# Attention with a lag of three steps: when the products with the values follow the scores, and where the rows of sums are kept

## The reference

```python
def attn(x, Wq, Wk, Wv, Wo, gamma, beta):          # x: 4 x 1024 x 256, 16 heads of 64
    q = jnp.einsum('bsd,hde->bhse', x, Wq)
    k = jnp.einsum('bsd,hde->bhse', x, Wk)
    v = jnp.einsum('bsd,hde->bhse', x, Wv)
    scores = jnp.einsum('bhse,bhte->bhst', q, k)
    scores = jnp.where(causal, scores / jnp.sqrt(jnp.float32(E)), -jnp.inf)
    out = jnp.einsum('bhst,bhte->bhse', jax.nn.softmax(scores, axis=-1), v)
    y = x + out.transpose(0, 2, 1, 3).reshape(B, S, H * E) @ Wo
    return layernorm(y, eps=1e-3) * gamma + beta

def ffn(x, w_gate, w_up, w_down):                  # integer weights times 1/127, 768 hidden
    return (silu(x @ wg.T) * (x @ wu.T)) @ wd.T

x = layernorm(x + attn(x, ...))
x = layernorm(x + ffn(x, ...))
```

## Time and profile before

| | |
|---|---|
| median of 3 runs | 1456.25 us (1454.54 to 1456.58) |
| the profiled execution, its own time | 1458.17 us |
| its span in the trace | 1456.4 us, mean granted clock 0.991 |
| busy: PE / PE weight loads / DVE / ACT / POOL | 97% / 85% / 71% / 69% / 68% of the span |
| instructions: PE / DVE / ACT / POOL | 7976 / 2747 / 1924 / 926 |
| chain that ended last, by engine | PE 73%, ACT 11%, DVE 8%, POOL 4%, issue 3%, DMA 1% |
| POOL's idle time before `probs_lo` (L1428) | 415.1 us, of it 412.5 until ACT's `probs_hi` |
| ACT's idle time before `probs` (L984) | 299.6 us, of it 217.8 until DVE's mask |

### The profile page before, as it was taken

The page is one execution under the profiler, slowest core; times in us unless marked ns, Lnnn a source line. Parts: engine busy times, 40 slices in busy tenths (PEclk is TensorE's granted clock), DMA queues, the critical chain, the costliest instruction groups (busy, mean ns, idle before and its releaser), DMA issues.

```text
span 1456.4 us, 23825 instructions
## 1 busy us (share of the span) xinstructions
PE 1409.0 (97%) x7976; PEld 1231.7 (85%) x7976; DVE 1031.7 (71%) x2747; ACT 1002.1 (69%) x1924; POOL 984.9 (68%) x926
## 2 busy tenths in 40 slices
PE   7899999999999999999999999999999999999876
PEld 6788888888888888888888888888888888888766
DVE  7777776767676766777667676776767677677864
ACT  4777777877676676867668676676767668676534
POOL 4665666556676775867768586775867768588744
PEclk9999999999999999999999999999999999999998
DMA  3323222323342132322243122132313223121000
GB/s 130 102 81 93 62 67 95 117 52 90 103 123 73 52 95 59 110 54 58 74 117 95 52 61 72 56 120 59 95 44 110 74 60 95 51 64 55 23 12 30
DMA packets 61241, 110.46 MB, mean 76 GB/s; under 512 B 16256, under 2 KB 41600, under 8 KB 61120
## 3 DMA queue, kind: packets, MB, share of 16 engines
q1 hardware_dynamic: 61120, 108.94, 25.2%
HBM read 60.95 MB, written 13.89 MB: 51 GB/s over the span
## 4 chain that ended last, share of the span: by engine, by line
PE 73%; ACT 11%; DVE 8%; POOL 4%; issue 3%; DMA 1%; SPq 0%; ACTq 0%; POOLq 0%
PE bank L798 22%; PE bank L771 15%; PE bank L671 8%; PE bank L747 8%; PE bank L734 7%; PE bank L696 5%; PE bank L833 5%; PE bank L845 3%; ACT probs_hi L987 2%; POOL probs_lo L1428 2%; ACT probs L984 2%; ACT y_tail L1023 1%; ACT Q L967 1%; POOL h_lo L1470 1%; ACT K L967 1%
## 5 line engine op out<-in xcount | busy, mean ns | idle before, releaser
L1428 POOL TENSOR_TENSOR probs_lo<-probs,probs_hi 128x512 fp32r<-128x512 f32 x576 | 747.6, 1305 | 415.1 <-ACT probs_hi L987 412.5
L984 ACT ACTIVATE probs<-bank 128x512 f32<-128x512 f32 x576 | 344.2, 598 | 299.6 <-DVE bank L1185 217.8
L771 PE MATMUL bank<-Q,K 128*128 128x512 f32 (+3 forms) x1536 | 385.9, 353 | 3.4 <-ACT probs_hi L987 2.6
L987 ACT ACTIVATE probs_hi<-bank 128x512 fp32r<-128x512 f32 x576 | 342.2, 594 | 0.0
L771 PEld LDWEIGHTS bank<-Q,K 128*128 128x128 f32 x1536 | 252.1, 190 | 33.6 <-ACT probs_hi L987 6.2
L747 PE MATMUL bank<-K,Q 128*128 128x512 f32 (+3 forms) x768 | 245.5, 362 | 3.9 <-DMA Q<-Q 3.3
L1169 DVE CUSTOM_DVE_ANT_0 bank<-bank,mask_keys_free 128x128 f32<-128x128 f32 (+3 forms) x512 | 243.2, 506 | 4.7 <-PE bank L747 4.2
L798 PE MATMUL bank<-probs_hi,VH 128*128 128x512 f32 (+3 forms) x768 | 232.6, 343 | 7.9 <-POOL probs_lo L1428 7.2
L798 PE MATMUL bank<-probs_lo,VH 128*128 128x512 f32 (+3 forms) x768 | 234.7, 346 | 0.0
L798 PE MATMUL bank<-probs_hi,VL 128*128 128x512 f32 (+3 forms) x768 | 234.7, 346 | 0.0
L1185 DVE TENSOR_TENSOR bank<-bank,mask_queries_free 128x256 f32<-128x256 f32 (+1 forms) x320 | 119.4, 373 | 129.4 <-PE bank L771 128.9
(11 more groups left out here) (173 smaller groups left out, 2230.9 us busy)
## 6 DMA issues: line engine op xcount, KB each, us to landing
Q<-Q SPq DMA_DIRECT2D x64, 256.0 KB, 3.7
K<-K SPq DMA_DIRECT2D x64, 256.0 KB, 3.6
recip_bc<-recip_scratch SPq DMA_DIRECT2D x62, 256.0 KB, 3.4
wh<-w_scratch SPq DMA_DIRECT2D x12, 768.0 KB, 4.3
wl<-w_scratch SPq DMA_DIRECT2D x12, 768.0 KB, 5.8
wo_quad<-wo SPq DMA_DIRECT2D x16, 256.0 KB, 2.9
y<-x SPq DMA_DIRECT2D x16, 256.0 KB, 3.8
x_tail<-x SPq DMA_DIRECT2D x13, 256.0 KB, 4.4
```

The lines of the kernel that those rows point to most:

```text
L771: last = mm(bk[:, at:at + cols], KX[:, n, P * i:P * i + P], QX[:, n, q0:q0 + cols], start=(KX is K1 and at == 0), stop=(KX is K2 and at + ...
L984: A(pe_[:, g % 2, :], stb[g % 2][:, :], ACT.Exp).then_inc(exp_done, 1)
L987: A(ph[:, g % RING, :], stb[g % 2][:, :], ACT.Exp).then_inc(hi_done, 1)
L1428: G.tensor_tensor(pl[:, g % RING, :], pe_[:, g % 2, :], ph[:, g % RING, :].bitcast(F32), ALU.subtract).then_inc(lo_done, 1)
```

## The change

- `LAG` goes from 2 to 3 and `RING` from 3 to 4: `pv(g)` is issued at step g + 3, and the tiles of high and low parts have four buffers each. For the last 18 pieces the lag stays 2 (`LAST_LAG`); at step `LAST_AT` + 2 two pieces are multiplied.
- The tile `row_sums` (4 KB in each partition) is gone, which is what the two further buffers take. An odd head's row of sums goes to row 64 of `recip_bc`, with a new wait for the scaling of the pair before. At the end, sums of the last heads go to the tile of a mask, with a wait for the last maximum.
- ACT's `copy_out` moves a step: first half from step 8 of a head to step 0 of the next, second half from step 2 to step 3. DVE's `recip` moves a step with `LAG`.
- SP's sums, stores and loads of reciprocals, one `dup_q` and the load of Wo move by one or two steps, and with it in its queue. `V_AT`, `V_LAST`, the projections, `max_bank` and the scaling stay where they are.

```diff
-LAG, RING = 2, 3
+LAG, RING = 3, 4
+LAST_LAG = 2
...
+def pv_due(g):
+
+    return [i for i, lag in ((g - LAG, LAG), (g - LAST_LAG, LAST_LAG)) if 0 <= i < NG and (i >= LAST_AT) == (lag == LAST_LAG)]
...
-        rsum, RB = sb("row_sums", [P, S]), sb("recip_bc", [P, S])
+        RB = sb("recip_bc", [P, S])
...
-                src = HT[E:E + 1, h // 2 % 3, :] if h % 2 == 0 else rsum[0:1, :]
+                src = HT[E:E + 1, h // 2 % 3, :] if h % 2 == 0 else RB[E:E + 1, :]
...
-                if s == 3 and 1 <= it < NIT:
+                if s == 4 and 1 <= it < NIT:
                     sums(QH * it - 1)
...
-                if s == 5 and 1 <= it < NIT:
+                if s == 6 and 1 <= it < NIT:
                     recip_store(QH * it - 1)
-                if s == 6 and 1 <= it < NIT:
+                if s == 8 and 1 <= it < NIT:
                     recip_load(QH * it - 1)
                 if s == 7 and live:
                     max_to_row(QH * it + 1)
                 if s == 7 and NQ <= nxt < NIT:
                     load_w(nxt)
-                if s == 12 and live:
+                if s == 13 and live:
                     sums(QH * it)
-                if s == 14 and live:
+                if s == 15 and live:
                     recip_store(QH * it)
-                if s == 15 and live:
+                if s == 17 and live:
                     recip_load(QH * it)
...
-                if 0 <= g - LAG < NG:
-                    pv(g - LAG)
+                for i in pv_due(g):
+                    pv(i)
...
                 if (n, c) == (HA, 0):
+
+                    act.wait_ge(mx_read, mx_event_t(NH - 1))
...
-                    A(rsum[own, cols], pvb[n - HA][other, :], ACT.Copy).then_inc(ht_copied, 1)
+                    A(maskS[own, :], pvb[n - HA][other, :], ACT.Copy).then_inc(ht_copied, 1)
...
                     if c == 0:
                         act.wait_ge(sums_loaded, 16 * h)
+                        act.wait_ge(ht_norm, 2 * pair)
+
                     A(HT[E:P, slot, cols], pvb[c][E:P, :], ACT.Copy)
-                    A(rsum[0:1, cols], pvb[c][0:1, :], ACT.Copy).then_inc(ht_copied, 1)
+                    A(RB[E:E + 1, cols], pvb[c][0:1, :], ACT.Copy).then_inc(ht_copied, 1)
...
-                if k == C0_DONE + LAG and 0 <= h < NH - 2:
-                    copy_out(h, 0)
+                if k == C0_DONE + LAG - NS and 1 <= h < NH - 1:
+                    copy_out(h - 1, 0)
```

More of the change, by code:

```diff
@@ L544, in last_recip_load @@
                 sp.wait_ge(recip_stored, 16 * (NH - 1))
-                sp.dma_start(rsum[0:E, CH:S], rscr[HA:HA + 1, 0:CH].partition_broadcast(E).rearrange("e o n -> e (o n)")).then_inc(recip_bc, 16)
+                sp.dma_start(RB[0:E, CH:S], rscr[HA:HA + 1, 0:CH].partition_broadcast(E).rearrange("e o n -> e (o n)")).then_inc(recip_bc, 16)
             def step(g):
@@ L553, in step @@
                         tail_store(XTRA if gset else n, n, gset)
-                if s == 2 and live:
+                if s == 3 and live:
                     dup_q(it, 1)
-                if s == 3 and 1 <= it < NIT:
+                if s == 4 and 1 <= it < NIT:
                     sums(QH * it - 1)
@@ L586, in step @@
                     dup_q(nxt, 0)
-                if s == 21 and live:
+                if s == 22 and live:
                     sums(QH * it + 1)
@@ L590, in step @@
                     dup_k(nxt, 0)
-                if s == 23 and live:
+                if s == 24 and live:
                     recip_store(QH * it + 1)
                     load_wo(it)
-                if s == 24 and live:
+                if s == 26 and live:
                     recip_load(QH * it + 1)
@@ L601, in step @@
                     y_init(it // NQ, Y_INIT_AT.index(s))
-                if s == 30 and 0 <= it < NIT - 1:
+                if s == 31 and 0 <= it < NIT - 1:
                     sums(QH * it + 2)
-                if s == 32 and 0 <= it < NIT - 1:
+                if s == 33 and 0 <= it < NIT - 1:
                     recip_store(QH * it + 2)
@@ L1067, in step @@
                 for h, c in ((NH - 2, 0), (NH - 1, 0), (NH - 2, 1)):
-                    if g == acc_done(h, c) + LAG + 1:
+                    if g == acc_done(h, c) + LAST_LAG + 1:
                         last_copy(h, c)
@@ L1319, in last_norm_c0 @@
                 dve.wait_ge(ht_copied, copies_before(NH - 1, 0) + 1)
-                V.reciprocal(rsum[:, cols], rsum[:, cols]).then_inc(last_recip, 1)
+                V.reciprocal(maskS[:, cols], maskS[:, cols]).then_inc(last_recip, 1)
                 dve.wait_ge(last_recip, 1 + q)
-                V.tensor_tensor(HT[:, slot, cols], HT[:, slot, cols], rsum[:, cols], ALU.mult).then_inc(last_norm, 1)
+                V.tensor_tensor(HT[:, slot, cols], HT[:, slot, cols], maskS[:, cols], ALU.mult).then_inc(last_norm, 1)
             def last_norm_c1(q):
@@ L1329, in last_norm_c1 @@
                     dve.wait_ge(recip_bc, 16 * (NH - 1))
-                    V.tensor_tensor(HT[0:E, slot, CH:S], HT[0:E, slot, CH:S], rsum[0:E, CH:S], ALU.mult)
+                    V.tensor_tensor(HT[0:E, slot, CH:S], HT[0:E, slot, CH:S], RB[0:E, CH:S], ALU.mult)
                     dve.wait_ge(pv_mm, acc_done(NH - 1, 1) + 1)
-                V.reciprocal(rsum[E:P, cols], pvb[HB - HA][0:E, here]).then_inc(last_recip, 1)
+                V.reciprocal(RB[E:P, cols], pvb[HB - HA][0:E, here]).then_inc(last_recip, 1)
                 dve.wait_ge(last_recip, 3 + q)
-                V.tensor_tensor(HT[E:P, slot, cols], pvb[HB - HA][E:P, here], rsum[E:P, cols], ALU.mult).then_inc(last_norm, 1)
+                V.tensor_tensor(HT[E:P, slot, cols], pvb[HB - HA][E:P, here], RB[E:P, cols], ALU.mult).then_inc(last_norm, 1)
             def step(g):
@@ L1368, in step @@
                     last_chain_recip()
-                if g == acc_done(NH - 1, 1) + LAG + 1:
+                if g == acc_done(NH - 1, 1) + LAST_LAG + 1:
                     last_norm_c1(0)
@@ L1388, in step @@
                 for q in range(2):
-                    if g == acc_done(NH - 1, 0) + LAG + 1 + q:
+                    if g == acc_done(NH - 1, 0) + LAST_LAG + 1 + q:
                         last_norm_c0(q)
-                if g == acc_done(NH - 1, 1) + LAG + 1:
+                if g == acc_done(NH - 1, 1) + LAST_LAG + 1:
                     last_norm_c1(1)
```

## The result

The changed kernel takes 1459.55 us (median of 17 runs, 1458.21 to 1463.21); the kernel before, run beside it, 1457.36 us (17 runs). The ratio of after to before is 1.0019, with a 95% interval of 1.0013 to 1.0026. By the ratio it is slower by 2.8 us (the medians differ by 2.2) where 6.7 less were forecast; that is just inside the 0.2% called "no change" ahead, but the interval does not hold 1.

A forecast was written before the change was run, and what follows sets the result against it. TensorE, busy 99.3 of 100 us, was taken as the bound, so only its waits could move the total. 7.2 us gained outside the eleven places and 0.5 lost in them gave -6.7: 1449.5 us, range 1445 to 1454 (1441 to 1460 with rivals).

The forecast's parts named there:

- The waits on POOL go: Products with the values: issued a step later, they lose all waits on POOL, 15.1 us, except 0.7 in the last eighteen steps.
- 7.2 us gained outside the eleven places: Waits on POOL removed everywhere except step 4 of iterations 5 to 15, the eleven places: 7.2 us gained.
- Rows of sums in the tile of the reciprocals: 0.: ACT's copies of the rows of sums: same two instructions to another tile, cost 0, bounds 0 and 1.9 us.
- the bound of 1.9: Upper bound in us on the cost of moving the rows of sums, from TensorE's present waits for copies.
- (a): Step 35: second V copy waits for products of its own step, +0.4 us; the first V copy's delay is hidden by this.
- (b): Step 0: Q copy 1.5 us later, DVE's rest of it ends at 1036.2, TensorE waits 0.3 us at the third projection.
- Sum (b) to (d): New waits at third projection, scores 4 and products behind the moved head copy: 0.65 us, against 0.66 that go at step 4.
- (d): Step 4: products wait 0.3 us for the copy of a head moved to step 3, which ends at 1043.05.
- +0.5 us over eleven iterations: Start of iterations 5 to 15: new waits replace the step-4 gain, net loss put at 0.5 us over the eleven.
- SP's queue: 0: Reciprocals' load behind the weights at step 8: between 0 and 1 us an iteration if 2 us late, taken as 0.
- the second one: Rival: exponential 35 and Q copy later than in (a); gain gone from 0.6 us more, 1462.8 at 1.2; chance 0.17.
- the third: Rival: reciprocals land 2 us late behind the weights, 1 us in each of 12 iterations, +5.3, 1461.6 us; chance 0.08.

The follow-up runs named there:

- e4: Kernel before, with only the odd heads' rows of sums put into the tile of the reciprocals, with the new wait: 1460.89 us, ratio 1.0022.
- e10: Kernel before, with the rows of sums in their own tile but at partition 64 instead of 0, no new wait: 1461.04 us, ratio 1.0028.
- e3: Changed kernel, with the first copy of a head and its row of sums behind the exponential of its step: 1458.91 us, ratio 1.0008 to the kernel before.
- e5: Changed kernel, with the copies of the values of steps 33 and 35 behind their exponentials: 1453.32 us, ratio 0.9974 to the kernel before.
- e12: Changed kernel, value copies of steps 33, 35 behind exponentials, weights behind reciprocals' load, projection-copy halves swapped, row of sums ahead of its head: 1447.54 us, ratio 0.9933.
- e11: Changed kernel, value copies of steps 33, 35 and step 3's copy of a head behind their exponentials, weights behind reciprocals' load: 1494.55 us, ratio 1.0258.
- e1: Changed kernel, with the next iteration's weights issued one step later, behind the load of the reciprocals: 1457.74 us, ratio 1.0000 to the kernel before.
- e9: Kernel before, with only the copies of the values of steps 33 and 35 behind their exponentials: 1466.59 us, ratio 1.0065.
- e13: Kernel before, with only the order of the two halves of each projection's copy swapped on ACT, and of DVE's rests: ratio 1.0000.

## Why the prediction was wrong

- *The waits on POOL go.* Right. Outside the last eighteen steps none is left at L804, and the copy of the head took the place at step 4 (0.28 to 0.30 us, counted from the starts).
- *7.2 us gained outside the eleven places.* Right. Iterations 0 to 4 gained 6.2 in spite of the 1.8 lost in iteration 3, and the 1.2 us of step 29 were kept: steps 27 to 35 of iterations 5 to 14 are 1.4 us shorter together.
- *"Rows of sums in the tile of the reciprocals: 0."* This step failed. Its reason, "the same two instructions, to another tile", left out where in the tile they write. On the kernel before it costs 0.31 us an iteration and 3.2 to 4.1 us in all (e4, e10); the bound of 1.9 was too low too, since it was taken from TensorE's waits for these copies and not from what stands behind them on ACT.
- *(a), the copies of the values.* Right in iteration 12, with the times counted from the scores of step 0. Exponential 34 is 0.84 us later than before (0.8 forecast), the second copy 0.36 (0.4 forecast), and the first copy's 2.94 us of idle time are hidden, as said: exponential 34 was done at 1029.01, and ACT still idled 0.64 us for the products of the second copy.
- *(b), the third projection, 0.3 us.* The mechanism was right, the size was not: it waits 0.76. The copy of Q is 1.75 us later instead of 1.5, 0.12 of it behind the row of sums and 0.15 behind the rows of the tail, where the copy of a head with its other first partition now follows. And the projection wants to start 0.12 us earlier than I took it, since the products ahead of it are those of piece 34, three matmuls where piece 35 had six (their last starts at 1034.63, and 0.23 later is 1034.86). The last 0.06 is the time from the end of DVE's rest to the projection's start.
- *Sum (b) to (d), "0.65 us against 0.66".* This step failed most: the sum ends at step 4, and what comes behind it stood at nothing without a reason. At step 4 itself (d) was near (in iteration 12 the products wait 0.30 us, 0.3 forecast). But at steps 5 and 6 TensorE waits 0.75 us an iteration more, for high parts and for DVE's maxima, 7.5 us in ten iterations, which is more than the 5.1 gained at step 4. What was taken for +0.5 us over eleven iterations is 8.1 us in ten. These later waits do not come from the copies of the values or from the late Q: they are as large in iteration 5, which waits nothing at the third projection, and they stay in e3 and e5; in e12, where those of step 5 are gone, those of step 6 stay. By the rows above they follow the copy of a head that moved to step 3, ahead of the copy of K. That was read from the traces and not tested alone (e11 moves that copy, but pays at step 4).
- *What the edits are worth.* Of the 0.9 us lost in an iteration, placing the copies of the values behind the exponentials gives 0.6 back (e5), and the row at partition 64 costs 0.3 on the kernel before (e4, e10). If the row costs as much in the changed kernel, which was not run, nothing of the loss is left, and the lag gives these iterations nothing either: what it gains at steps 4 and 29 goes, but for about 1 us in ten iterations, to steps 5 and 6.
- *SP's queue: 0.* Nearly right. In iteration 12 the load was issued at 1051.12, and POOL scaled at 1057.99 where 1056.9 was forecast. The Trainium skill's rule on the order of a ring ("DMA: Bandwidth & Descriptors", queues, rings and completion order) agrees with this trace: behind the weights the load took 6.9 us where it had taken 3.8. POOL's wait is hidden, as said; only in iteration 3, where DVE scales and wo follows at once, did it reach TensorE: 1.8 us (e1).
- *The rivals.* By its price it was the second one, ACT at the start of an iteration: 0.9 us an iteration, between its 0.6 and 1.2. But that the price fits is partly luck. Its condition was that exponential 35 and the copy of Q come later than in (a), and they did so by 0 and 0.25 us; most of the rest came up at steps 5 and 6. Of the third there was a part, in iteration 3 alone. That the total moved by only 2.8 us is a sum of terms that cancel.

The sum, put right: -6.2 in iterations 0 to 4 (with 1.8 lost to the load), +8.1 in 5 to 14, +1.8 behind them: +3.7, against spans of 1456.4 and 1460.0. Not tried is the lag of three with the rows still at partition 0 of a tile of their own: the fourth buffer has taken that room. Left open is why the last iteration loses 1.8 us: 1.1 lie in its steps 0 to 6 and so look like the others, 1.0 behind the last scores, which was not tested.

## What to carry to other kernels

When a stage is moved a step later, list everything on every engine that waits for it: a wait for an older step was free here, a wait for the same step stopped ACT's whole queue, and whether to put it behind the step's urgent work depends on what else stands there (e5 against e9). Then do the same for everything that the moved work now stands ahead of. Follow a delay on a full engine until that engine has idled again, not just to the first place where it is waited for. A late producer that is hidden in one iteration can be bare in one that has another consumer.

## What the runs showed of the hardware

On ACT the time from one instruction to the next depended on the partitions of both. With 512 columns per partition, from start to start: 0.49 to 0.50 us where both read and write from the same first partition (the row of sums at partition 0, then Q, V or an exponential, 60 places in the kernel before), and 0.60 to 0.62 where the first partition of source or destination changes between 0 and 64 (62 places of the row behind its head, 60 of the row at 64 ahead of the next copy in the changed kernel, both halves of every projection). The duration drawn is 0.59 to 0.60 in both. Taking two changes of five out at each of two places in an iteration gave 0.41 us of 0.48 worked out (e12); moving one without taking it out gave nothing (e13). What in the engine makes the difference these runs do not tell.
